# A graph network on one Trainium2 core: who adds x, who copies the turned rows, and where the bias is added in layer 2's node stage

## What is computed

```python
y = relu(layernorm(x))
h = y @ w_nbr
agg = segment_sum(edge_weight[:, None] * h[src], dst)
x = x + agg + y @ w_own + bias
```

## Time and profile before

| | us |
|---|---|
| median of three runs | 6020.4 (6016.84 to 6021.12) |
| the profiled execution's own time | 6016.64 |
| its span, first to last instruction | 6014.9 |
| TensorE busy | 4348.8 (72%) |
| VectorE busy | 4179.2 (69%) |
| GpSimd busy | 3617.6 (60%) |
| ScalarE busy | 2463.8 (41%) |
| mean granted TensorE clock | 0.832 of full |

### The profile page before, as it was taken

The page is one execution under the profiler, slowest core; times in us unless marked ns, Lnnn a source line. Parts: engine busy times, 40 slices in busy tenths (PEclk is TensorE's granted clock), DMA queues, the critical chain, the costliest instruction groups (busy, mean ns, idle before and its releaser), DMA issues. The chain is left out here.

```text
span 6014.9 us, 78255 instructions
## 1 busy us (share of the span) xinstructions
PE 4348.8 (72%) x17463; PEld 2676.3 (44%) x17463; DVE 4179.2 (69%) x9983; ACT 2463.8 (41%) x6920; POOL 3617.6 (60%) x4190
## 2 busy tenths in 40 slices
PE   2799999999995665566567777777856666666596
PEld 1544444444474444444343433344434444444385
DVE  5599999999975556555555555555657766776766
ACT  2498888988853333333320000000113333333343
POOL 3465555555526777777567777777357777775001
PEclk9899999999987777777777677777877777777898
DMA  6453333333335555555333333333235555553301
GB/s 166 162 160 98 98 98 98 97 99 97 98 106 148 140 143 145 141 141 144 110 98 105 105 106 105 105 105 105 95 106 147 148 144 146 147 147 106 100 0 44
DMA packets 468850, 699.69 MB, mean 116 GB/s; under 512 B 212924, under 2 KB 310800, under 8 KB 468262
## 3 DMA queue, kind: packets, MB, share of 16 engines
q0 software_dynamic: 171200, 474.81, 28.4%
q1 hardware_dynamic: 284336, 207.07, 11.9%
q10 hardware_dynamic: 12896, 13.11, 0.6%
HBM read 620.77 MB, written 70.10 MB: 115 GB/s over the span
## 5 line engine op out<-in xcount | busy, mean ns | idle before, releaser
L275 POOL DMA_INDIRECT G<-table,srcI x1760 | 1673.6, 951 | 582.7 <-issue 497.9
L544 PE MATMUL pS<-G,one 128*128 128x260 f32 (+1 forms) x3520 | 1203.6, 480 | 192.2 <-issue 96.2
L1421 POOL DMA_INDIRECT G<-table,srcI x880 | 830.1, 943 | 600.1 <-ACT zt L1445 545.3
L1557 PE MATMUL pM<-zt,one 128*128 128x512 f32 x1760 | 945.2, 618 | 113.3 <-DVE zt L1503 73.7
L477 ACT ACTIVATE acc<-pS x1760 | 691.7, 393 | 779.3 <-PE pS L544 519.5
L625 POOL DMA_INDIRECT G<-table,srcI x880 | 833.5, 947 | 280.9 <-issue 149.0
L661 PE MATMUL pM<-G,one 128*128 128x256 f32 x1760 | 790.5, 555 | 254.7 <-issue 132.5
L1445 ACT ACTIVATE zt<-G,a4S 128x128 f32<-128x128 f32 x2640 | 856.9, 390 | 0.0
L544 PEld LDWEIGHTS pS<-G,one 128*128 128x128 f32 x3520 | 593.0, 212 | 263.3 <-issue 210.1
L661 PEld LDWEIGHTS pM<-G,one 128*128 128x128 f32 x1760 | 374.0, 255 | 657.5 <-DVE one L634 515.3
L641 DVE TENSOR_TENSOR acc<-acc,pM 128x256 f32 x880 | 370.4, 421 | 393.4 <-PE pM L661 388.6
(11 more groups left out here) (326 smaller groups left out, 5907.1 us busy)
## 6 DMA issues: line engine op xcount, KB each, us to landing
G<-table,srcI POOLq DMA_INDIRECT x3520, 2.8
relT<-step_rel SPq DMA_DIRECT2D x220, 256.0 KB
a10T<-step_a SPq DMA_DIRECT2D x660, 30.0 KB
far<-step_rec SPq DMA_DIRECT2D x224, 64.0 KB
table<-row SPq DMA_DIRECT2D x100, 128.0 KB, 1.7
acc<-zero SPq DMA_DIRECT2D x21, 512.0 KB, 5.1
step_a<-part SPq DMA_DIRECT2D x7, 960.0 KB
table<-row SPq DMA_DIRECT2D x50, 132.0 KB, 1.7
```

Source lines behind the costliest of these rows:

```text
L275: pool.indirect_dma_start(G[:, par * C + j, 0:ROW], None, tab, bass.IndirectOffsetOnAxis(ap=srcI[:, k:k + 1], axis=0)).then_inc(s_g[par * ...
L544: nc.tensor.matmul(sum_of(of[j]), one[:, par * C + j, :], G[:, par * C + j, :], start=False, stop=True, skip_group_check=True).then_inc(s_ ...
L1421: pool.indirect_dma_start(G[:, k % GS, :], None, table[0], bass.IndirectOffsetOnAxis(ap=srcI[:, k:k + 1], axis=0)).then_inc(s_g[k % GS], 16)
L1557: nc.tensor.matmul(pM[k % 2][:, :], one[q % 2][:, s, :], z_of(q)[:, s, :, :], start=True, stop=True).then_inc(s_m, 1)
```

## The change

In layer 2's node stage the sum with x moves from GpSimd to VectorE: `Layer1End.plus` is called on VectorE two tiles ahead of the statistics, and `second` does nothing. With `turn_on_act=True` the turned rows are copied by ScalarE, between norm of n and copy-out of n-2, and not by VectorE. The bias sum of VectorE and the load of the bias, repeated over 128 partitions, go; in the pass the bias is loaded as one row, and a product of a row of ones with it opens each of the 50 own products in PSUM.

```diff
--- before.py
+++ after.py
@@ -596,7 +596,7 @@
                         opened(pS[:, 0, 511:512])
                         over_chunks(pe, chunk)
 
-        def edge_sum(u, rows, acc, hT, w_own):
+        def edge_sum(u, rows, acc, hT, w_own, bias):
 
             with Stage() as se:
                 G = [se.sb(f"G{j}", [P, D]) for j in range(u)]
@@ -604,7 +604,7 @@
                 one = [se.sb(f"one{j}", [P, P]) for j in range(R)]
                 pM = [se.ps(f"pM{j}", [P, D]) for j in range(R)]
                 pO = [se.ps(f"pO{j}", [P, D]) for j in range(2)]
-                w_sb = se.sb("w_sb", [P, 2, D])
+                w_sb, b_sb = se.sb("w_sb", [P, 2, D]), se.sb("b_sb", [1, D])
                 s_w, s_o = se.sem("s_w"), se.sem("s_o")
                 EVERY = K // NT
 
@@ -649,10 +649,11 @@
                     @block.sync
                     def _(sp):
                         sp.dma_start(w_sb[:, :, :], w_own.rearrange("(c p) n -> p c n", p=P)).then_inc(s_w, 16)
+                        sp.dma_start(b_sb[:, :], bias.rearrange("(a n) -> a n", a=1)).then_inc(s_w, 16)
 
                     @block.tensor
                     def _(pe):
-                        pe.wait_ge(s_w, 16)
+                        pe.wait_ge(s_w, 32)
 
                         def scatter(k, j):
                             pe.wait_ge(s_one, k + 1)
@@ -662,8 +663,9 @@
                             n = own_at(k)
                             if n is not None:
                                 freed(pe, s_acc, added(EVERY * (n - 1) - 1) + 1 if n >= 2 else 0)
+                                nc.tensor.matmul(pO[n % 2][:, :], ones[0:1, :], b_sb[0:1, :], start=True, stop=False)
                                 for c in range(2):
-                                    ins = nc.tensor.matmul(pO[n % 2][:, :], hT[:, n, c * P:(c + 1) * P], w_sb[:, c, :], start=(c == 0), stop=(c == 1))
+                                    ins = nc.tensor.matmul(pO[n % 2][:, :], hT[:, n, c * P:(c + 1) * P], w_sb[:, c, :], start=False, stop=(c == 1))
                                 ins.then_inc(s_o, 1)
                         steps(pe, u, (0, scatter))
 
@@ -741,7 +743,7 @@
         GT = 5
 
         def node_stage(layer, x_sb, rstd, shift, wide, load, biases, act_end, dve_end, store, RW=D, keep=None,
-                       finish=None, saved=None, beside=None):
+                       finish=None, saved=None, beside=None, turn_on_act=False):
 
 
 
@@ -850,6 +852,10 @@
                             nc.scalar.activation(y[j][:, :], tile(x_sb, n), ACT.Relu, bias=shift[:, ds(n, 1)],
                                                  scale=rstd[:, ds(n, 1)]).then_inc(s_y, 1)
 
+                        def turned(n, j):
+                            act.wait_ge(s_t, n + 1)
+                            nc.scalar.activation(turned_rows(n, j), pT[j][:, :], ACT.Copy).then_inc(s_yt, 1)
+
                         def end(n, j):
                             act.wait_ge(s_o, n + 1)
                             freed(act, s_st[j], 8 * n_st * (n - j))
@@ -859,6 +865,8 @@
                                 finish.scalar(act, n + AH + 6)
                             if 0 <= n < NT:
                                 norm(n, n % 2)
+                            if turn_on_act and 0 <= n - 1 < NT:
+                                turned(n - 1, (n - 1) % 2)
                             if 0 <= n - 2:
                                 end(n - 2, n % 2)
 
@@ -889,7 +897,8 @@
                             if 0 <= n < NT:
                                 if beside is not None:
                                     beside.lowest(dve, n)
-                                turned(n, n % 2)
+                                if not turn_on_act:
+                                    turned(n, n % 2)
                             if 0 <= n - 2 and dve_end is not None:
                                 end(n - 2, n % 2)
 
@@ -1726,32 +1735,34 @@
                 def vector(self, dve, n):
                     if 0 <= n + 4 < NT:
                         self.first(n + 4)
+                    if 0 <= n + 2 < NT:
+                        self.plus(dve, n + 2)
 
                 def first(self, n):
                     heads = acc[:, n, 0:D].rearrange("p (h f) -> p h f", h=H1)
                     nc.vector.tensor_tensor(heads, heads, self.den[:, n, :].unsqueeze(2).broadcast_to([P, H1, F1]), ALU.mult).then_inc(self.s_over, 1)
 
+                def plus(self, dve, n):
+                    dve.wait_ge(self.s_over, n + 1)
+                    dve.wait_ge(self.s_xr[n % self.R], n // self.R * 16 + 16)
+                    nc.vector.tensor_tensor(acc[:, n, 0:D], acc[:, n, 0:D], self.xr[n % self.R][:, :], ALU.add).then_inc(self.s_plus, 1)
+
                 def second(self, pool, n):
-                    pool.wait_ge(self.s_over, n + 1)
-                    pool.wait_ge(self.s_xr[n % self.R], n // self.R * 16 + 16)
-                    pool.tensor_tensor(acc[:, n, 0:D], acc[:, n, 0:D], self.xr[n % self.R][:, :], ALU.add).then_inc(self.s_plus, 1)
+                    pass
 
                 def ready(self, dve, n):
                     dve.wait_ge(self.s_plus, n + 1)
 
             def act_end(act, n, j, pO, row, aux):
                 return nc.scalar.activation(row[:, :], pO[0][:, :], ACT.Copy)
-
-            def dve_end(dve, n, j, pO, row, aux, s_ae, b):
-                return nc.vector.tensor_tensor(tile(x_sb, n), tile(x_sb, n), b[1][:, :], ALU.add)
 
             with Stage() as st2:
                 hT = st2.sb("hT2", [P, NT, D])
                 node_stage(2, x_sb, rstd, shift, [D],
-                           lambda w, b: [(w[0][:, :, :], a["L2_gnn_w_nbr"].rearrange("(c p) n -> p c n", p=P)),
-                                         (b[1][:, :], a["L2_gnn_bias"].rearrange("(a n) -> a n", a=1).broadcast_to([P, D]))],
-                           [0, D], act_end, dve_end, [(lambda n: table[2][ds(n * P, P), :], lambda row, aux: row[:, :])], keep=hT, finish=Layer1End())
-                edge_sum(U2, table[2], x_sb, hT, a["L2_gnn_w_own"])
+                           lambda w, b: [(w[0][:, :, :], a["L2_gnn_w_nbr"].rearrange("(c p) n -> p c n", p=P))],
+                           [0], act_end, None, [(lambda n: table[2][ds(n * P, P), :], lambda row, aux: row[:, :])], keep=hT, finish=Layer1End(),
+                           turn_on_act=True)
+                edge_sum(U2, table[2], x_sb, hT, a["L2_gnn_w_own"], a["L2_gnn_bias"])
 
 
             F3 = D // H3
```

## The result

The changed kernel takes 5974.55 us in the median of four runs (5964.68 to 5979.65), the kernel before beside them 6018.62 us: 44 us less, a ratio of 0.9927 (95% interval 0.991 to 0.9944). The profiled execution is the longest of the four, 5979.65 us.

What follows compares the result with a forecast made beforehand. GpSimd's single queue, 9.1 us of scales and sums per five tiles, was taken to bound layer 2's node stage. At 1.22 us a tile the stage saves 45.1 us: 6020.4 - 45.1 = 5975.3, rounded to 5975 us; range 5966 to 5999.

Steps and rivals of the forecast that it cites:

- way round through the statistics: Node stage: the rest of a five-tile group's 10.8 us beyond GpSimd's 9.1 us of scales and sums.
- Part 1: Node stage: VectorE adds x at 0.33 us each, 16.5 us in all; the new wait for x loads costs nothing.
- as long as today: Stage opening: first copy-out stays at 3017.0; five statistics stand behind 21 VectorE operations, 6.9 us.
- rival 1: Node stage: another queue binds, VectorE awaiting x loads or its sums slowing scales; 1.7 us a tile, 5999 us, chance 0.24.
- Part 2: Node stage: ScalarE copies turned rows at 0.38 us each; its chain takes 2.43 us for two tiles, 1.22 a tile.
- The low clock: Node stage's first tiles: TensorE products take 2.08 us, not 1.18, adding 1.4 us over three tiles.
- Part 3: Bias moved into the pass: 50 products priced at nothing under GpSimd's gathers; 43 to 63 us if that cover failed.
- The sum: Node stage: 3017.0 + 49 x 1.22 + 1.4 puts the last copy-out at 3078.2, 45.1 us less.
- 2: Node stage: clock stays low, about 2.1 us a tile, 3 us saved, 6017 us, chance 0.06.
- 3: Pass: TensorE sets the pace, bias products add 63 us, so slower at 6038 us, chance 0.05.
- 4: Node stage: stores, not GpSimd's sum, set the pace; 1.58 us a tile, 29 us saved, 5991 us, chance 0.13.
- three signs of being wrong: Stage and pass: scales over 6 us a group, VectorE waiting for loads by the dozen, or gathers waiting for TensorE.

Runs made afterwards that it cites:

- the run with the turned copy and bias alone: Changed kernel with the sum with x back on GpSimd: 7032.35 us against 7054.73 for the kernel before, ratio 0.9970.
- the run with more buffers: Changed kernel with 28 buffers for x in place of 20: 5984.79 us against 6017.84 for the kernel before, ratio 0.9944.
- ten bias products: Changed kernel with ten bias products ahead of each own product in the pass, not one: 5978.31 us against 6021.82 for the kernel before, ratio 0.9931.
- x alone: Kernel before with only the sum with x moved to VectorE: 7030.99 us against 7054.73, ratio 0.9969.
- The deeper buffers: Changed kernel with three PSUM product buffers and four row buffers in layer 2's node stage, not two each: 5975.82 us against 6021.82 before, ratio 0.9923.

## Why the prediction was right

**The bound before.** Right: GpSimd's single queue held the pace, by 9.1 us a group. The "way round through the statistics" was seen in size and not in cause; the run with the turned copy and bias alone shows it is VectorE's backlog of turned copies and bias sums behind the stop.

**Part 1.** VectorE's sums stand 0.33 us apart, as priced. The new wait for x was priced at nothing and took 12.4 us in 21 stops without norm ever waiting: right, and by the scales of the run with more buffers perhaps even a help. The term that was mis-sized is "as long as today" for the opening: the 21 operations took the 7 us as forecast (the scales begin 9.0 us behind the stage's start, 8.8 before), but the first scales took 8.53 us for 5.13. That is rival 1's clash, in the one place where VectorE runs without a wait. The Trainium skill (SBUF, State Buffer, section "Who interferes with whom") says that a VectorE instruction with two SBUF inputs contends with a GpSimd instruction that reads SBUF. The trace agrees that they clash, 0.57 to 0.87 us for 0.20; the run with the weights on ScalarE, where such an instruction got by with 0.30, shows that the pair alone does not fix the price. Behind the opening the scales took 4.9 to 6.0 us a group, under the 6.1 from which rival 1 would decide.

**Part 2.** A forecast of 1.22 us a tile stands against 1.19 (3059.58 to 3079.85, seventeen tiles), and the chain is the one that was named: priced at 2.43 us for two tiles, it takes 2.37. The low clock cost 0.6 us and not 1.4. Two long gaps, 3.1 us over the cadence, were not foreseen.

**Part 3.** Nothing, as priced: gathers at 0.949 us with 0.30 us between, first to last 1102.6 us, and 1100.2 to 1100.7 in the four runs with a bias product whose gathers took 946 ns, against 1100.4 before. GpSimd's gap of 0.30 us a gather was the right ground to choose nothing and not 63 us. TensorE's busy time between the first and last gather grew from 851 to 881 us, by 30 and not by 40 to 60. In the pass the bias product stands as a group of its own (line 666), here with the gathers:

```profile
L625 POOL DMA_INDIRECT G<-table,srcI x880 | 835.6, 950 | 282.7 <-issue 158.2 <-PE pM L662 109.8 <-ACTq L620 14.8
...
L666 PE MATMUL pO<-b_sb,ones 1*128 1x256 f32 x100 | 55.9, 655 | 0.0
```

**The sum.** From first to last copy-out 61.2 us were forecast and 62.2 measured; the last falls at 3080.7 and not 3078.2. The stage gave 42.0 us where 45.1 were forecast, 3.1 short: 2.3 in the opening and 1.0 between the copy-outs, less 0.1 behind the last. So the mechanism and the size are right to about 3 us; that the median, 5974.55, lies within 0.5 us of the forecast is luck, for the runs of the kernel alone spread over 15. In the profiled execution the span fell by 37.0 us only: of the stage's 42.0, 2.2 us are lost in layer 2's pass and 3.5 behind it, and 0.7 were gained ahead of the stage. The pass's gathers took 949 ns each in the median and not 946, in layer 0's pass too (947 for 944), which the change does not touch; the second profile of the same kernel has 947. That is the runs' own spread, not a cost of the change.

**The rivals.** 1 shows in the opening alone. 2: the clock was 0.99 behind the opening. 3: excluded by ten bias products. 4: the stores did not set the pace; their waits came from the turned copy and the bias sum in VectorE's queue (23.7 us with these left there, 3.2 with these gone and GpSimd's stop kept) and fell to 3.8 us.

**The signs.** The prediction named three signs of being wrong, and read by the letter all three came while it held: scales over 6 us a group (8.53 and 6.01 for the first two), waits for loads by the dozen (21), and gathers that wait for TensorE (109.8 us, but 118.8 before as well). They counted waits and not what a wait costs: norm stood for scales only once. ScalarE was also not the busiest engine of the stage, with 56.5 us against TensorE's modelled 62.6, and the scales began 6.5 us apart in the mean, not 6.

## What to carry to other kernels

When an in-order engine stops for another, count what is queued behind the stop and whom that serves: here VectorE's stop cost more than its length because the next round's input came last in its backlog. Relieving one overloaded queue pays only until the next one holds: x alone gave 24 us and left VectorE's five operations a tile, the rest alone gave 23 and left GpSimd's 9.1 us a group, both together gave 42. Here a dense run of two-input VectorE operations slowed GpSimd's small chain by two thirds, and moving the chain only moved the slow group; giving a part of the two-input operations to an idle engine removed it in the one run that tried, for a reason that is open. And write a sign of being wrong as a wait that costs something, not as a wait that exists.

## What the runs showed of the hardware that was not expected

- Small GpSimd instructions of 5 columns, 0.20 us each, took 0.57 to 0.87 us beside back-to-back two-input VectorE operations, while VectorE's kept 0.40 to 0.41 us; in one run, with the weights of twelve tiles on ScalarE, none of the small ones in the first two groups took over 0.43. Before, GpSimd's large sums had made VectorE's take 0.94.
- With 450 more products in the pass the granted clock was 0.77 and not 0.70, and the pass was some 2 us longer at most.
- The two long gaps stand at nearly the same places of the program in both profiles of the changed kernel. Before each, one issue on SP is slow: a load's takes 1.17 and 0.87 us for 0.43 in the first profile; in the second it is a store's, 1.18 for 0.32, and then a load's, 0.69. A store then lands late:

```profile
3035.73 1.17 SPq L1713 DMA_DIRECT2D xr<-x  x1
...
3037.87 0.38 ACT L1757 ACTIVATE row<-pO 128x256 f32<-128x256 f32 x1 [1.77 <-DMA table<-row]
```

  The deeper buffers hide it: that run has a slow issue too (1.05 us) and no long gap. What causes it is open; no run here was made for it.
